# A mixture-of-experts stage begins: VectorE's tables in another order, half a store ahead of a weight load

## What is computed

```python
def _L0_ffn_ref(x, gate_w, gate_b, w1, w2, w3):
    logits = jnp.einsum('bsd,de->bse', x, gate_w) + gate_b
    probs = jax.nn.softmax(logits, axis=-1)
    top_probs, top_idx = jax.lax.top_k(probs, 2)
    top_probs = top_probs / jnp.sum(top_probs, axis=-1, keepdims=True)
    dispatch = jnp.sum(jax.nn.one_hot(top_idx, n_experts, dtype=x.dtype) * top_probs[..., None], axis=-2)
    h1 = jnp.einsum('bsd,edh->bseh', x, w1)
    h2 = jnp.einsum('bsd,edh->bseh', x, w2)
    hidden = jax.nn.silu(h1) * h2
    expert_out = jnp.einsum('bseh,eho->bseo', hidden, w3)
    return jnp.einsum('bseo,bse->bso', expert_out, dispatch)

x = x + _L0_gnn_ref(_layernorm(x, axis=-1), L0_gnn_weight, L0_gnn_bias, edge_index, edge_type_8)
x = x + _L0_ffn_ref(_layernorm(x, axis=-1)[None], L0_ffn_gate_w, L0_ffn_gate_b, L0_ffn_w1, L0_ffn_w2, L0_ffn_w3)[0]
```

## Time and profile before

| | us |
|---|---|
| median of 3 runs | 914.04 |
| lowest and highest | 911.89, 915.19 |
| the profiled execution | 916.64 |
| its span on the core | 914.8 |
| start of tile 0's `up` | 588.80 |
| start of tile 6's `up` | 628.35 |
| end of the last tile's work on PE, about | 890 |

### The profile page before, as it was taken

One profiled execution on the slowest core, in us unless ns is written; L12 is line 12 of the kernel. 1 busy time (PEld: TensorE's weight loads), 2 busy tenths in 40 slices (PEclk: granted clock), 3 DMA queues, 4 the chain that ended last, 5 costly groups with the idle time before them and its releaser, 6 DMA issues.

```text
span 914.8 us, 19945 instructions
## 1 busy us (share of the span) xinstructions
PE 731.6 (80%) x4626; PEld 623.0 (68%) x4627; DVE 518.1 (57%) x1444; ACT 302.4 (33%) x469; POOL 655.4 (72%) x609
## 2 busy tenths in 40 slices
PE   0136697888788898888879888689999999999980
PEld 0125586777677676777758676467888888788870
DVE  6887566545556446555446767874444444344438
ACT  5524234332333323343233523122333333233323
POOL 7777777777777777777777740359787886987772
PEclk9998799999999999999979998999999999999995
DMA  9875656433333333333364324176656655663546
GB/s 203 250 229 179 189 184 199 142 106 105 106 107 108 107 105 105 106 108 105 108 187 132 104 65 167 30 266 200 212 189 218 229 184 187 200 215 93 163 133 187
DMA packets 92526, 142.09 MB, mean 155 GB/s; under 512 B 13752, under 2 KB 67069, under 8 KB 92476
## 3 DMA queue, kind: packets, MB, share of 16 engines
q0 software_dynamic: 25440, 69.50, 26.1%
q1 hardware_dynamic: 50114, 56.92, 19.6%
q10 hardware_dynamic: 16922, 15.15, 5.2%
HBM read 108.59 MB, written 32.93 MB: 155 GB/s over the span
## 4 chain that ended last, share of the span: by engine, by line
PE 45%; POOL 22%; issue 14%; DMA 10%; DVE 7%; ACT 1%; DVEq 0%; POOLq 0%; SPq 0%; ACTq 0%
POOL got L611 20%; PE ps L1759 16%; PE ps L1741 9%; PE ps L1593 8%; PE ps L1605 6%; DMA got<-x_tab,gidx 6%; PE ps L1767 3%; DMA store<-in_L_gnn_weight 2%; PE ps L1725 1%; PE ps L1694 1%; DVE ps L1510 1%; POOL part L617 1%; DMA y_tab<-ffn 1%; DMA part<-in_x,early_idx 1%; POOL part L645 1%
## 5 line engine op out<-in xcount | busy, mean ns | idle before, releaser
L611 POOL DMA_INDIRECT got<-x_tab,gidx x383 | 366.4, 957 | 118.3 <-issue 108.9
L1593 PE MATMUL ps<-hot,got 125*128 125x256 f16 x1680 | 219.3, 290 | 79.7 <-DMA got<-x_tab,gidx 75.7
L1593 PEld LDWEIGHTS ps<-hot,got 125*128 125x128 f16 x1680 | 170.1, 104 | 122.9 <-issue 38.4
L1156 DVE TENSOR_TENSOR store<-store,ps 128x512 f32 x150 | 102.6, 684 | 179.2 <-PE ps L1593 146.2
L1759 PE MATMUL ps<-part,operands 128*128 x696 | 179.3, 407 | 4.9 <-DVE operands L1432 3.1
L1605 PE MATMUL ps<-part,store 128*128 128x256 f32 x800 | 181.9, 386 | 0.5 <-DVE acc L1167 0.5
L1605 PEld LDWEIGHTS ps<-part,store 128*128 128x128 f32 x800 | 152.5, 193 | 20.7 <-issue 0.6
L1759 PEld LDWEIGHTS ps<-part,operands 128*128 128x128 f32 x696 | 128.3, 191 | 32.5 <-issue 5.7
L1138 DVE TENSOR_SCALAR hot<-key_row,pass,drel 125x256 f16<-125x256 f16 x425 | 126.1, 362 | 7.5 <-ACT store L778 4.9
L1741 PE MATMUL ps<-part,operands 128*128 x696 | 97.9, 289 | 3.8 <-DVE operands L1442 3.6
L645 POOL TENSOR_TENSOR part<-store,part 128x2048 fp32r<-128x2048 f32 (+1 forms) x28 | 98.0, 3500 | 2.3
(11 more groups left out here) (254 smaller groups left out, 685.8 us busy)
## 6 DMA issues: line engine op xcount, KB each, us to landing
store<-in_L_ffn_w SPq DMA_DIRECT2D x48, 512.0 KB, 4.8
part<-x_tab SPq DMA_DIRECT2D x625, 1.0 KB
y_tab<-ffn SPq DMA_DIRECT2D x9, 896.0 KB, 6.3
y_tab<-ffn ACTq DMA_DIRECT2D x58, 128.0 KB
xs_tab<-x_sb SPq DMA_DIRECT2D x14, 512.0 KB, 3.3
ffn<-xs_tab ACTq DMA_DIRECT2D x55, 128.0 KB
got<-x_tab,gidx POOLq DMA_INDIRECT x383, 2.8
acc<-in_x SPq DMA_DIRECT2D x5, 560.0 KB
```

The lines of the kernel that those rows point to most:

```text
L611: nc.gpsimd.indirect_dma_start(got[:, c, :], None, x_tab, bass.IndirectOffsetOnAxis(ap=gidx[:, col:col + 1], axis=0)).then_inc(gathered[g] ...
L1156: v.tensor_tensor(window, window, ps[:, WIN_BANK[g], :].rearrange("p (q n) -> p q n", n=WIN), ALU.add).then_inc(win_added, 1)
L1593: last = mm(ps[:, WIN_BANK[g], k * KEYS:(k + 1) * KEYS], rows, hot[0:CE, g % HOT, c - c0, :], start=(c == c0 and a == 0), stop=(c == c1 - ...
```

## The change

Three parts.

1. On DVE the same table steps stand in other places. `rank` and the first product with `t_off` come ahead of `low_xs(0)`, `positions` ahead of `order_tables`. `split_first(0, (DOWN_PART,))` comes behind tile 0's product, `split_first(1, ...)` between tile 1's `low_hid` and its product, `oct_tables` behind tile 1. `slots_needed` and `result_weights` are cut in pieces and stand in the tiles 2, 3 and 4.
2. On SP the first half of octet 0 is stored, and has landed, before the weights of expert 2 are loaded; the second half follows behind them.
3. On ACT the rows of tiles 4 and 5 are asked for behind the work of tile 2, not behind those of tiles 1 and 2. ACT's loop now starts one pair later and the pair stands written out.

```diff
+            def store_half(q, n):
+
+                sp.wait_ge(oct_got[n], (q + 1) * HALF_OCT * 16)
+                sp.sem_inc(tiles_begun, 1)
+                sp.dma_start(xs_tab[bass.ds((q * 2 + n) * HALF_OCT * P, HALF_OCT * P), :].rearrange("(t p) d -> p t d", p=P),
+                             xg[:, n * HALF_OCT:(n + 1) * HALF_OCT, :]).then_inc(xs_stored, 16)
+                sp.wait_ge(xs_stored, (q * 2 + n + 2) * 16)
+                sp.sem_inc(tiles_begun, 1)
...
             sp.wait_ge(order_done, 1)
+            store_half(0, 0)
             load_next(2, 0)
-            store_oct(0)
+            store_half(0, 1)
             sp.wait_ge(owner_done, 4)
...
             expert_tile(0, 0, first=True)
-            expert_tile(0, 1, second=True)
-            with act.Fori(1, early + (LAST_PAIRS - 1)) as i:
+            expert_tile(0, 1, second=True, load=False)
+            expert_tile(1, 0, load=False)
+            load_xs(DIRECT, 0)
+            load_xs(DIRECT + 1, 1)
+            expert_tile(1, 1)
+            with act.Fori(2, early + (LAST_PAIRS - 1)) as i:
...
+            def offset_hots(hot_k):
+
+                step(v.tensor_tensor(hot_k, hot_k, bc(t_off[:, :], TE, 1), ALU.mult))
+
             def positions():
 
-                for hot_k in (hot1, hot2):
-                    step(v.tensor_tensor(hot_k, hot_k, bc(t_off[:, :], TE, 1), ALU.mult))
...
-                step(v.tensor_reduce(rank[:, :], smaller[0:1, :, :], AX.X, ALU.add))
...
+            step(v.tensor_reduce(rank[:, :], smaller[0:1, :, :], AX.X, ALU.add))
+            offset_hots(hot1)
             low_xs(0)
+            offset_hots(hot2)
+            positions()
             order_tables()
-            positions()
-            split_first(0, (DOWN_PART,))
...
+            def early_slots():
+
+                rows_upto(0)
+                rows_upto(1)
+
+            def early_weights():
+
+                slots_needed()
+                result_weights()
+
-            expert_tile(0, 0, first=True, tables=oct_tables)
-            split_first(1, (UP_PARTS, DOWN_PART))
-            expert_tile(0, 1, tables=slots_needed)
-            result_weights()
-            expert_tile(1, 0)
-            expert_tile(1, 1)
-            expert_tile(2, 0)
+            expert_tile(0, 0, first=True)
+            split_first(0, (DOWN_PART,))
+            expert_tile(0, 1, tables=lambda: split_first(1, (UP_PARTS, DOWN_PART)))
+            oct_tables()
+            expert_tile(1, 0, tables=early_slots)
+            expert_tile(1, 1, tables=early_weights)
+            expert_tile(2, 0, tables=sorted_weights)
             expert_tile(2, 1)
```

More of the change, by code:

```diff
@@ L542, in _ @@
             store_x2(X_LOADS - 1)
+            def store_half(q, n):
[5 more added lines that the diff above has]
+                sp.sem_inc(tiles_begun, 1)
             def store_oct(q):
                 for n in range(2):
-                    sp.wait_ge(oct_got[n], (q + 1) * HALF_OCT * 16)
-                    sp.sem_inc(tiles_begun, 1)
-                    sp.dma_start(xs_tab[bass.ds((q * 2 + n) * HALF_OCT * P, HALF_OCT * P), :].rearrange("(t p) d -> p t d", p=P),
-                                 xg[:, n * HALF_OCT:(n + 1) * HALF_OCT, :]).then_inc(xs_stored, 16)
-                    sp.wait_ge(xs_stored, (q * 2 + n + 2) * 16)
-                    sp.sem_inc(tiles_begun, 1)
+                    store_half(q, n)
             sp.sem_inc(xs_stored, 16)
@@ L1454, in expert_tile @@
                 v.tensor_tensor(hid, gate, ps[:, UP_BANK + 1, :], ALU.mult).then_inc(hid_ready, 1)
-                if first and tables:
-                    tables()
                 low_xs(j + 1)
@@ L1462, in _, with rows_upto @@
             pairs = dve.value_load(pairs_i[0:1, 0:1], min_val=EXPERTS // 2, max_val=SLOT_TILES // 2)
+            step(v.tensor_reduce(rank[:, :], smaller[0:1, :, :], AX.X, ALU.add))
+            offset_hots(hot1)
             low_xs(0)
+            offset_hots(hot2)
+            positions()
             order_tables()
-            positions()
-            split_first(0, (DOWN_PART,))
+            def rows_upto(k):
+                dve.wait_ge(upto_kept, 2)
+                step(v.tensor_tensor(mine, upto_tile, bc(same[:, EXPERTS - 2 + k, :], [1, TILES, EXPERTS], 1), ALU.mult))
+                step(v.tensor_reduce(upto[:, k, :], mine, AX.X, ALU.add))
             def slots_needed():
-                dve.wait_ge(upto_kept, 2)
-                tile_row = [1, TILES, EXPERTS]
-                for k in range(2):
-                    step(v.tensor_tensor(mine, upto_tile, bc(same[:, EXPERTS - 2 + k, :], tile_row, 1), ALU.mult))
-                    step(v.tensor_reduce(upto[:, k, :], mine, AX.X, ALU.add))
                 step(v.tensor_scalar(upto_i[:, :, :], upto[:, :, :], float(P - 1), None, ALU.add))
@@ L1490, in result_weights, with sorted_weights @@
                 step(v.tensor_tensor(wts[:, 1, :], wts[:, 1, :], wts[:, 0, :], ALU.mult))
+            def sorted_weights():
                 for k in range(2):
```

## The result

The changed kernel takes 922.4 us (median of 6 runs, 919.3 to 925.7), the kernel before 914.6 beside it (911.9 to 916.5): 0.85% slower, ratio 1.0085 with a 95% interval of 1.0062 to 1.0108. The forecast was 918.0, with 920.2 as the upper end. The direction and the place were right, the size was not: 7.8 us instead of 4.0.

The account below looks back on a forecast made before the run. PE and POOL were taken to hold most of the chain, with POOL's split setting tile 6. Tile 6 +2.45 and clock +1.6 gave +4.0 us: span 918.8 against 914.8, median 918.0 against 914.04, range 912.6 to 920.2.

Parts of the forecast that it names:

- upper end: Slowest time of the range, 920.2 us: second store landed at 614.1, tile 6 +3.65 us, clock loss 2.4 us.
- The tables: VectorE's moved table steps at the first tiles: Silu at 590.8, tiles 2 to 4 some 5.5 us earlier.
- The stretched gather: POOL's fourth gather, started inside VectorE's two-input operation, ends at 598.15 and lands at 599.95; such gathers take 2.3 to 2.5 us.
- first rival: POOL's gathers are not stretched: weights at 602.4, second half at 610.8, together +2.0 us; chance 0.27.
- the term of the landing: Second half's store behind the third expert's weights on SP's queue: lands at 612.9 against 608.7, 4.2 us later.
- upper bound of 9.3: Latest landing of the second half's store: 9.3 us after 604.8, at 614.1, with the slower set of weights.
- POOL's slack of 1.75: At tile 6, POOL's split would allow a start at 626.6 instead of 628.35; at most 1.75 us of PE's gain passes.
- The clock: PE's matmuls after its wait before tile 6 run slow at the lower clock: +1.6 us, between 0 and 2.4.
- late stall: PE's wait of 1.79 us at tile 38, ending with POOL's split of an expert's weights; said to follow PE.
- No queue: Second store overtakes the weights on SP's queue, landing at 609.1: +0.2 us, or -1.35 without clock loss; chance 0.14.
- PE's lead survives: POOL does not hold tile 6, so tile 4's 5.4 us gain reaches the end: 908.6 us; chance 0.07.
- ScalarE's row loads: Tile 4's rows there by 606.5, wanted at 609: no cost, or up to 3 us ahead of tile 6 behind weights.

Follow-up runs that it names:

- w1_only: The changed kernel, but only w1 (0.5 MB) of the third expert's weights loaded between the two half stores, w2 and w3 behind the second: ratio 1.003.
- load_last3: The changed kernel with both half stores ahead of the third expert's weights: 914.67 against 913.98 us, ratio 1.001.
- no_sp3: The changed kernel with SP's old order, weights ahead of both half stores; tables and row loads stay moved: 917.69 against 913.98 us, ratio 1.0031.
- act_back: The changed kernel with ScalarE's two row loads back in their old places: ratio 0.9999, on chips where the kernel before takes 1205 us.
- pool_swap: The changed kernel with POOL splitting the third expert's weights ahead of its second gathers: ratio 0.9985, on chips where the kernel before takes 1205 us.
- load_last_only: The kernel before with only SP's order changed, both half stores ahead of the third expert's weights: ratio 1.0005.
- gathers_first: The changed kernel, but the third expert's weights are loaded only after the second half's gathers have landed: ratio 1.0088.
- swap_load_last: The changed kernel with both half stores ahead of the third expert's weights and POOL splitting those weights ahead of its second gathers: ratio 1.005.

## Why the prediction was right in direction and short in size

In us after tile 0's start:

| step | predicted | measured |
|---|---|---|
| ScalarE's first Silu | 2.0 | 1.9 |
| tile 1, tile 3, tile 4 | 4.7, 17.0, 22.2 | 4.8, 17.1, 22.3 |
| weights of the third expert issued | 15.7 | 15.8 |
| second half's store issued | 17.2 | 17.4 |
| second half landed | 24.1 | 26.8 |
| tile 6 | 42.0 | 44.5 |
| slow matmuls behind the wait | +1.6 | +1.9 |

**The tables** did what the rows said for PE, and their lead of 5.6 us was lost at tile 6, as predicted.

**The stretched gather** came where it was put: the fourth, begun inside the 2.27 us operation, took 2.54 us. It was the condition of the forecast against its first rival, and it held here; in w1_only the sixth was stretched and the first half was stored 3.5 us earlier. So this term changes from execution to execution.

**The failed step** is the term of the landing. I put the second half 8.4 us behind the first weight load, from 7.1 for an undisturbed set of weights and 1.5 for the store behind it, or by bytes at 366 GB/s. It took 10.9 (602.18 to 613.1), above even my upper bound of 9.3. The bytes were about right (2.35 MB estimated, 2.48 moved from 603 to 613); the rate was not. The mean over this set was 248 GB/s: it ran at 301 and 240 until 608 and reached 348 only behind that. The 366 of the earlier trace rows was no lucky stretch, for the set in the kernel before has a mean of 343 over eight microseconds, and with that the sum by bytes would have grown by 0.4 us alone. So the step that failed is to carry the rate and the landing of the old place over to the new one; why the same loads are slower there stays open. That is 2.5 us, and all of it passes tile 6, because POOL's slack of 1.75 was already spent: copy +6.8 less 1.75 is 5.1, measured 4.98.

At that place the prediction set the figures of the Trainium skill ("DMA: Bandwidth & Descriptors", section Bandwidth: 435 GB/s at the fabric, about 358 as HBM's share) beside the row's. Both are ceilings; the trace's mean of 248 GB/s lies well below either, and neither prices a store that shares its queue with 1.5 MB of loads.

**The clock** fell as forecast, and cost 1.9 us (2.1 to 2.3 in load_last3 and no_sp3). What I didn't see: at the late stall it did not fall, 1.6 us back. With it the profiled execution is 5.5 us later behind tile 0, and the medians are 7.8 apart. The 2.3 us between are not in the trace that I have; its execution was the fastest of six, and whether the others had the slow tile behind the late stall or a later landing isn't known. So of the 3.8 us by which the predicted difference is short, the landing is 2.5, the clock 0.3 and tile 21 0.3, the late stall gives 1.6 back, and 2.3 are open. The time before tile 0 can't be told apart either: it is 586.4 to 590.0 us in the eight traces of undisturbed chips.

**The rivals.** No queue, and PE's lead survives, are out by the 9.4 us and the 10.52 us wait. The 922.4 us lie above the upper end, 920.2 (whose own terms add up to 920.1), which held a landing 9.3 us behind the first load. ScalarE's row loads, priced at nothing, cost PE nothing at tile 4, which came on time; whether they slow the weights act_back doesn't decide, and in no_sp3 they lie beside the store, where the sum might have needed a term for them.

## What to carry to other kernels

Before a load is moved on a queue, list what is issued behind it on the same queue and who waits for that: here a 0.5 MB store that a neighbour engine needs went from 3 to 9 us behind 1.5 MB that its reader wanted only 10 us after that store, and with the load issued last the kernel was as fast as before (1.001). A lead won upstream is worth only the slack of the next meeting point; ask which engine sets that before reordering for it. A rate read at one place is an estimate at another: the same 1.5 MB ran among transfers of 343 GB/s before and of 248 after, so give such a term a range that holds both. Try each part of a change also in the other part's new order, since here the tables set when the store began. Repeat a gain measured on an unusual chip before believing it.

## What the runs showed of the hardware

A gather that POOL issues beside VectorE's 2.27 us operation on two inputs in SBUF takes 2.3 to 2.55 us instead of 0.95, and ends some 0.8 us behind that operation. In w1_only (VectorE, POOL):

```profile
594.36 2.28 DVE L1396 TENSOR_TENSOR part<-store,part 128x2048 fp32r<-128x2048 f32 x1
594.94 2.52 POOL L662 DMA_INDIRECT x_sb<-x_tab,oct_idx  x1 [0.31 <-issue]
```

The Trainium skill ("SBUF — State Buffer", section Who interferes with whom) infers that such an operation doesn't stall descriptor generation, the work by which POOL issues a DMA; every trace of this case shows the gather held. A gather also reads its row numbers from SBUF (`oct_idx`), so that reading may be what is held; no run here separates the two.

The other way round VectorE is held: beside POOL's subtraction of 4.50 us in pool_swap the step on `wts` and `mtx` took 4.46 us instead of 0.18, and beside that of 2.34 us 2.30 (rows above).

A store on another queue is late as well. ScalarE stored a result at 603.65 in the changed kernel, and VectorE's copy that waits for its landing started 8.2 us later:

```profile
611.86 0.42 DVE L1448 COPY ffn<-ps 128x256 f32<-128x256 f32 x1 [3.42 <-DMA y_tab<-ffn]
```

The late stall of PE, 1.1 to 1.8 us, was followed by a slow tile (6.45 to 6.49 us) in before, no_sp3, load_last3 and load_last_only, and by one of 4.9 us in after, w1_only, gathers_first and swap_load_last. PE idled 1.78 to 1.81 us in the first four and 1.13 to 1.77 in the others. The longer waits are the slow ones, but only 0.01 us lies between the nearest two, and no run changed this wait alone. What decides stays open.
